# The late half of the diagonal: scored first and added on GpSimd instead of multiplied on its own

## The reference, cut to what matters

```
q, k = x @ Wq, latent_kv @ W_up_k ; v = latent_kv @ W_up_v      # B = 2, S = 1024, D = 128
scores = einsum('bhqd,bhkd->bhqk', qh, kh) * scale
scores = scores * exp(-0.0001 * |q_pos - k_pos|)                # decay by distance
out    = einsum('bhqk,bhkd->bhqd', softmax(scores), vh)
```

## Time and profile before

| what | value |
|---|---|
| median of 3 runs | 1040.08 us |
| the runs | 1040.08, 1025.58, 1045.73 us |
| the profiled execution | 1036.77 us, its span 1035.1 us |
| mean granted TensorE clock | 0.858 of full speed |
| busy in the span | PE 803.2, PEld 471.5, DVE 646.0, ACT 452.2, POOL 206.9 us |
| layer 0's attention groups | about 99 to 515 us of the span |

### The profile page before, as it was taken

How to read it: one execution, slowest core, us unless ns; L and a number is a source line. 1 busy time by engine, 2 the same in 40 slices (tenths; PEclk the granted TensorE clock), 3 DMA queues, 4 the chain that set the end, 5 groups by cost and what they waited for, 6 DMA issues and landing times. The chain is left out here.

```text
span 1035.1 us, 22868 instructions
## 1 busy us (share of the span) xinstructions
PE 803.2 (78%) x9457; PEld 471.5 (46%) x9457; DVE 646.0 (62%) x1922; ACT 452.2 (44%) x646; POOL 206.9 (20%) x218
## 2 busy tenths in 40 slices
PE   6374998999989999999754765999997793137960
PEld 3001554455545555554443653666664362025750
DVE  3784787689877989891053144667676545742427
ACT  5510576477757677778731232334332312001210
POOL 3980121111212121122204420000000000025330
PEclk9555799699989999999975887999999896558985
DMA  6535105031423231000084113700000001001014
GB/s 187 144 136 136 52 8 90 2 68 32 63 35 55 44 60 40 4 3 4 3 261 120 33 60 119 240 2 1 1 1 0 3 1 41 0 19 39 21 31 116
DMA packets 46217, 58.76 MB, mean 57 GB/s; under 512 B 7540, under 2 KB 24893, under 8 KB 46112
## 3 DMA queue, kind: packets, MB, share of 16 engines
q1 hardware_dynamic: 42992, 51.47, 19.2%
q0 software_dynamic: 2304, 4.59, 1.6%
q10 hardware_dynamic: 816, 1.23, 0.4%
HBM read 42.07 MB, written 14.94 MB: 55 GB/s over the span
## 5 line engine op out<-in xcount | busy, mean ns | idle before, releaser
L821 DVE CUSTOM_DVE_ANT_0 junk<-row,rest 128x512 bf16<-128x512 f32 x448 | 295.4, 691 | 62.8 <-PE row L421 61.8
L641 ACT ACTIVATE prob<-score 128x1024 f32<-128x1024 f32 x256 | 253.2, 1026 | 107.1 <-PE score L421 106.9
L421 PE MATMUL row<-stack 72*32 72x512 bf16 x1792 | 183.2, 399 | 5.1 <-issue 3.0
L421 PE MATMUL score<-stack 75*32 75x512 bf16 (+3 forms) x2816 | 163.2, 332 | 18.7 <-DMA stack<-neg_rows 9.8
L509 PE MATMUL out_ps<-prob,v_aug 128*32 128x256 f32 x2048 | 157.7, 392 | 0.0
L421 PEld LDWEIGHTS score<-stack 75*32 75x32 bf16 x2816 | 69.2, 98 | 86.9 <-issue 19.7
L722 POOL TENSOR_SCALAR_AFFINE_SELECT prob<-prob 128x512 f32<-128x512 f32 x64 | 40.7, 636 | 303.4 <-ACT prob L641 303.4
L421 PEld LDWEIGHTS row<-stack 72*32 72x32 bf16 x1792 | 48.7, 97 | 67.5 <-DVE top L821 44.0
L509 PEld LDWEIGHTS out_ps<-prob,v_aug 128*32 128x32 f32 x2048 | 62.7, 114 | 34.0 <-issue 4.9
L1393 PE MATMUL up_ps<-rows_t,up_w 128*128 128x320 f32 (+1 forms) x192 | 64.4, 465 | 14.0 <-issue 7.0
L1845 PE MATMUL outs<-vm_w,mixed 128*128 128x256 f32 x256 | 62.4, 387 | 1.8 <-issue 1.7
(11 more groups left out here) (298 smaller groups left out, 1132.1 us busy)
## 6 DMA issues: line engine op xcount, KB each, us to landing
stack<-parts_dram SPq DMA_DIRECT2D x288, 64.0 KB
parts_dram<-prob SPq DMA_DIRECT2D x12, 256.0 KB, 2.2
parts_dram<-stack SPq DMA_DIRECT2D x12, 256.0 KB, 3.5
results<-empty SPq DMA_DIRECT2D x12, 256.0 KB, 3.4
up_w<-in_L_ffn_w_dram SPq DMA_DIRECT2D x1, 2048.0 KB, 11.1
rows<-x_tok SPq DMA_DIRECT2D x8, 256.0 KB, 3.3
rows_in<-results SPq DMA_DIRECT2D x8, 256.0 KB, 4.2
up_w<-in_L_ffn_wg_dram SPq DMA_DIRECT2D x1, 2048.0 KB, 12.1
```

Source lines behind the costliest of these rows:

```text
L421: last = pe.matmul(out[c:c + 32, :], keys[:, c:c + 32], queries, start=True, stop=True)
L641: act.activation(prob[tile % 2][:, h, :], score[n % 2][:, :], ACT.Exp).then_inc(exped, 1)
L821: dve.tensor_tensor_reduce(junk[:, n % 2, :], row[:, n % 2, :], rest[:, at:at + HALF], 1.0, LOWEST, ALU.mult, ALU.max, top[:, 0, h, tile, ...
```

## The change

The late unit of a pair is put ahead of the pair's eight tile units. Its masked blocks are no longer multiplied by the values on PE. POOL masks a tile's diagonal blocks as before and then adds the pair's masked late blocks into them (fp32, 128 x 512 a tile, into `prob`), and signals `joined`. The tile's last weighing turn waits for `joined` in place of `masked`; ACT's next write to the late buffer waits for `joined` in place of the late product. `weigh_late` and its schedule entries go, so the schedule has 69 steps and NW is 8.

```diff
         for pair in range(SB // 2):
+            units += [("late", pair, 0)]
             units += [("tile", 2 * pair + k, h) for k in range(2) for h in range(GH)]
-            units += [("late", pair, 0)]
...
-            if kind == "tile" and tile > 1 and tile % 2 and h == 0:
-                schedule.append(("late", tile // 2 - 1, 0))
-        tail = [("weigh", SB - 1, turn) for turn in range(4)] + [("late", SB // 2 - 1, 0)]
+        tail = [("weigh", SB - 1, turn) for turn in range(4)]
...
-        NW = len(product_order)
+        NW = SB
...
-        def used_late(g, pair):
+        def joined_late(g, pair):
             if pair >= 2:
-                return g.n * NW + product_order.index(("late", pair - 2)) + 1
-            return (g.n - 1) * NW + product_order.index(("late", SB // 2 - 2 + pair)) + 1
+                return g.n * SB + 2 * (pair - 2) + 2
+            return (g.n - 1) * SB + 2 * (SB // 2 - 2 + pair) + 2
...
                     if turn == 3:
-                        pe.wait_ge(masked, g.n * SB + tile + 1)
+                        pe.wait_ge(joined, g.n * SB + tile + 1)
...
-                def weigh_late(g, pair):
-                    pe.wait_ge(mask_late, g.n * (SB // 2) + pair + 1)
-                    for k in range(2):
-                        tile = 2 * pair + k
-                        for h in range(GH):
-                            last = pe.matmul(out_ps[32 * h:32 * h + 32, tile * P:(tile + 1) * P],
-                                             v_aug[g.third][:, tile, h, :], prob_late[pair % 2][:, k, h, :],
-                                             start=False, stop=(pair == SB // 2 - 1), skip_group_check=True)
-                    last.then_inc(weighted, 1)
...
                             if not (first(g) and tile < 2):
-                                act.wait_ge(weighted, used_late(g, tile))
+                                act.wait_ge(joined, joined_late(g, tile))
...
+                        elif h == GH - 1:
+
+                            block = prob[tile % 2][:, :, tile * P:(tile + 1) * P]
+                            pool.wait_ge(exped, g.n * NU + n + 1)
+                            pool.affine_select(out=block, in_=block, compare_op=ALU.is_ge, fill=0.0, base=0,
+                                               pattern=[[0, GH], [1, P]], channel_multiplier=-1).then_inc(masked, 1)
+                            pool.wait_ge(mask_late, g.n * (SB // 2) + tile // 2 + 1)
+                            pool.wait_ge(masked, g.n * SB + tile + 1)
+                            pool.tensor_tensor(block, block, prob_late[tile // 2 % 2][:, tile % 2, :, :], ALU.add).then_inc(joined, 1)
```

More of the change, by code:

```diff
@@ L215, in attention @@
         neg_in = [sem(f"neg_in{i}") for i in range(3)]
-        scored, exped, masked, mask_late = sem("scored"), sem("exped"), sem("masked"), sem("mask_late")
+        scored, exped, masked, mask_late, joined = sem("scored"), sem("exped"), sem("masked"), sem("mask_late"), sem("joined")
         weighted, o_copied, o_turned, o_inv, o_done = sem("weighted"), sem("o_copied"), sem("o_turned"), sem("o_inv"), sem("o_done")
@@ L277, in attention @@
                      for key, order in orders.items()}
-        product_order = [(kind, tile) for kind, tile, turn in schedule + tail if kind == "late" or (kind == "weigh" and turn == 3)]
-        product_order = [("tile" if kind == "weigh" else kind, tile) for kind, tile in product_order]
-        NW = len(product_order)
+        NW = SB
         def used_tile(g, tile):
             if tile >= 2:
-                return g.n * NW + product_order.index(("tile", tile - 2)) + 1
-            return (g.n - 1) * NW + product_order.index(("tile", SB - 2 + tile)) + 1
-        def used_late(g, pair):
+                return g.n * NW + tile - 1
+            return (g.n - 1) * NW + SB - 1 + tile
+        def joined_late(g, pair):
             if pair >= 2:
-                return g.n * NW + product_order.index(("late", pair - 2)) + 1
-            return (g.n - 1) * NW + product_order.index(("late", SB // 2 - 2 + pair)) + 1
+                return g.n * SB + 2 * (pair - 2) + 2
+            return (g.n - 1) * SB + 2 * (SB // 2 - 2 + pair) + 2
         def judged_first(eng):
@@ L510, in weigh @@
                                          v_aug[g.third][:, tile, h, :], prob[tile % 2][:, h, at:at + S // 4],
-                                         start=(tile == 0 and turn < 2), stop=False, skip_group_check=True)
+                                         start=(tile == 0 and turn < 2), stop=(tile == SB - 1 and turn >= 2), skip_group_check=True)
                     if turn == 3:
                         last.then_inc(weighted, 1)
-                def weigh_late(g, pair):
-                    pe.wait_ge(mask_late, g.n * (SB // 2) + pair + 1)
-                    for k in range(2):
-                        tile = 2 * pair + k
-                        for h in range(GH):
-                            last = pe.matmul(out_ps[32 * h:32 * h + 32, tile * P:(tile + 1) * P],
-                                             v_aug[g.third][:, tile, h, :], prob_late[pair % 2][:, k, h, :],
-                                             start=False, stop=(pair == SB // 2 - 1), skip_group_check=True)
-                    last.then_inc(weighted, 1)
                 def turn_out(g):
@@ L552, in body @@
                                 turn_neg(nxt)
-                        elif kind == "weigh":
+                        else:
                             weigh(g, tile, h)
-                        else:
-                            weigh_late(g, tile)
                 run_groups(pe, body)
@@ L623, in finish @@
                 def finish(g):
-                    act.wait_ge(weighted, (g.n + 1) * (SB + SB // 2))
+                    act.wait_ge(weighted, (g.n + 1) * NW)
                     if not first(g):
@@ L717, in body @@
                     for n, (kind, tile, h) in enumerate(units):
[L718 to L724, removed]
                         if kind == "late":
```

## The result

| | median of 20 runs | lowest to highest |
|---|---|---|
| before | 1032.72 us | 1020.92 to 1047.85 |
| changed | 1036.74 us | 1026.93 to 1045.12 |

A forecast was written before the change was run, and what follows sets the result against it. PE was taken as the bound at full clock, with DVE only 6% behind. The terms -6.3 + 2.1 + 0.7 + 0.9 + 1.4 gave -1.2 us, 1035.6 on the profiled run, forecast at 1037; 8-in-10 range 1020 to 1051.

The forecast's parts named there:

- My own sign of being wrong: At a group's end, output copy beginning later than T + 8.5 us, T being the last row unit on PE.
- the groups of 58 rows: Four groups with 58 row units, each forecast 1.1 us shorter (4.4 in all) as late products leave PE.
- DVE's two-input instructions: POOL's add slows two subtractions in DVE's negated-maxima chain: +0.2 us a group, 7 times, +1.4; row maximum priced 0.
- The end of a group: From the last row unit to the output copy, the cover hiding the late mask is used up: +0.1 us, 7 groups, +0.7.
- Late products leave PE: 32 late products of 0.44 us leave PE, 14.1 at most; DVE's row pacing leaves -6.3 us together.
- The late unit at the start: Pair 0's late unit is new at a group's start, where exponentials outlast PE's step: 0.3 x 7 = +2.1 us.
- The last group: ACT ends it; after the last exponential, mask, add, waits and product take 2.8 us against 1.86 before: +0.9.
- POOL's add: 1.27 us each, 64 times, 81 us on POOL, 10 a group: hidden, with 30 us to spare.
- rival 3: The add also holds DVE's row maximum (line 821): about +70 us, 1106; chance 0.04.
- Rival 1: Full gain: doubled row units fill holes in DVE, nearly all 14.1 us come off, 1023 to 1027; chance 0.16.
- Rival 4: The extra late unit's wait and the joins eat all gain and more: +1 us a group, 1045; chance 0.05.
- Rival 2: PE's unexplained stalls, guessed as instructions running dry behind stack loads, move: 1019 without both, 1053 with two more; chance 0.15.

The follow-up runs named there:

- e1: The changed kernel with POOL's add for tile 6 held until DVE has finished the negated maxima; ratio to the kernel before 1.0022 (0.9978 to 1.0065).
- e8: The changed kernel with tile 6's add replaced by a one-input POOL mask of about the same length; no total time or ratio given.
- e11: The kernel before with a one-input POOL copy of 896 columns added across DVE's negated-maxima steps in each group but the last; ratio 1.0001 (0.9953 to 1.0049).
- e3: The changed kernel without POOL's add, the masked late blocks left out of the result; ratio 0.9981 (0.9949 to 1.0013).
- e2: The kernel before with the late unit at the start of its pair, late products still on PE, no add; ratio 1.0005 (0.9961 to 1.0050).
- e12: The kernel before without the stack loads of groups 3 to 7; ratio 0.9913 (0.9873 to 0.9952).
- e5: The kernel of e1 with tile 7's late blocks multiplied on PE instead of added by POOL; ratio 0.9996 (0.9964 to 1.0028).
- e4: The changed kernel with RESERVE 11 in place of 13, row units spread over 58 of 69 steps; ratio 1.0060 (1.0019 to 1.0100).
- e6: The kernel of e5 with RESERVE 12, the last row unit one step later; ratio 1.0107 (1.0051 to 1.0163).
- e10: The kernel before, unchanged, run again for a second trace; against itself in that comparison 0.9953 (0.9917 to 0.9988).

## Why the prediction was wrong

Forecast: -1.2 us on the profiled execution. Undisturbed groups say about +0.15 in kind A (-0.2 against the second trace of the kernel before, 52.57), +0.4 in B and +0.85 in C, twice each, +0.55 for the last, and in the first group's end +1.4 (copy at T + 8.73 in place of T + 7.35), which its stretch before T may partly give back (its length hangs on how long the clock stayed low at the start, and differed by 11 us between traces): 2.7 to 4.8 us. The medians differ by 4.0. The timed intervals are +4.1 to +10.5 us and -0.8 to +7.5; if the first is taken at its middle, 2 to 5 us of it are not explained by the groups. My own sign of being wrong, a copy later than T + 8.5, came true (8.95); the groups of 58 rows, which I had about 1 us shorter, are 0.4 to 0.85 longer. Step by step:

- *DVE's two-input instructions: the step that failed in its mechanism.* I priced +0.2 a group, through two subtractions, and said that the transpose had 0.3 of room. The instruction held was the cast between them, with one input in SBUF (the subtraction behind it kept its 0.19), and the transpose came 0.57 late, all of it paid by the group: 4 us in place of 1.4 (e1, e8, e11). I had taken from the row-maximum rows that one SBUF input is safe. Those rows show that for an instruction that reads PSUM and SBUF, and nothing for casts and tensor_scalars within SBUF. The Trainium skill's page "SBUF — State Buffer", section "Who interferes with whom", has this case: an instruction with one SBUF input keeps clear of GpSimd only outside the 2-port modes; copy, cast and tensor_scalar can run in such a mode, and then whichever of VectorE and GpSimd issues first blocks the other fully until it ends. The traces agree: the casts and the tensor_scalar that started behind POOL lasted until POOL's end (1.14, 0.95 and 1.12 us in place of 0.18). In which mode they ran no run shows.
- *The end of a group: mis-sized.* I compared with T + 8.04, which is kind A's. The ends before were 8.04, 8.43 and 7.75, and 7.35 in the first group. Without the cast's part (e1) they are 8.38, 8.38 and 8.15, and 8.15: +0.34, -0.05, +0.4, +0.8, together 2.2 us in place of 0.7. In e1 the last exponential ended at T + 5.5, where I had 5.3, and the copy came 2.9 behind it, where I had 2.6.
- *Late products leave PE: right in kind, too large.* In seven groups 3 to 3.6 us came off (e3 against e2), where my figures give 5.0 for the same seven and 6.3 for all with the stretches at half clock. That DVE's row pacing holds the rest fits: in kind B up to T, PE's row loads waited 6.7 us for DVE in e3, 5.1 in e2. The miss is in kinds B and C, where the part from the copy to T shrank by 0.62 us and I had 1.1; in kind A it shrank by 0.7 in one group and 0.1 in the other, and I had 0.3.
- *The late unit at the start:* +0.47 before T in each group where I had 0.3, but most of it came back at the end (e2), +0.1 to +0.2 a group in all.
- *The last group:* +0.55 in place of +0.9.
- *POOL's add:* 1.28 us, hidden, the row maximum untouched: right, and rival 3 is out. (Its sum had an error: 81 us less 448 times 0.04 is +63, not +70.) Rival 1 is out too: without any add e3 was at best 5 us below the kernel before by its timed interval. Rival 4, which I gave 0.05, is the one that came, smaller than its +1 a group. Rival 2: the stalls are real, move from run to run, and are what I took them for (e12). In the four traces of the two kernels they do not account for the difference; in the timed runs this was not measured.

Of PE's busy time I said 1.7 us a group less. It fell by 0.8 to 0.9 in undisturbed groups; I read this as overlap, since products that overlap leave less busy time than their starts suggest.

## What to carry to other kernels

Before moving work to GpSimd, list what VectorE runs at that moment in SBUF alone: casts, copies and scalar steps of 0.2 us wait out a GpSimd instruction of 1.3 us, and a short chain on the critical path is where that hurts, however idle GpSimd looks. Count such a chain's room in each kind of loop body, not in one. And where two engines are within 6% of each other, taking work from one gains what the other leaves: here 3 to 3.6 of 12.3 us, less than the 4 that one new wait at each group's end took back.

## What the runs showed of the hardware

- A GpSimd instruction that reads and writes SBUF held DVE's cast (fp32 to bf16) and tensor_scalar, both of 128x32 and within SBUF, until it ended: 0.79 to 1.15 us in place of 0.18. An add with two inputs, a mask with one and a copy with one all did so. A tensor_scalar that had started 0.02 us before the add kept its 0.18. The 128x512 maximum with one input from PSUM was not held (690 ns).
- PE's waits within a group for nothing that the profile shows, 1 to 3.6 us, came behind late packets of the queue of kind "instruction": 10 to 15 us apart in place of about 7, while the stack loads ran. PE went on 2.6 to 3.3 us after the late packet's start, in all 16 cases. Without those loads neither the gaps nor the waits were there (e12). Such a gap did not always make PE wait (e3, e5: gaps of 11 to 14 us, no wait of 1 us).
- The granted clock fell to 0.5 (1.2 GHz) behind some of PE's waits and not behind others: for 17 us from the last microsecond of the 3.26 us wait of the kernel before, for 17 us behind one of 0.67 us in e4, for 10 to 24 us behind those of 0.94 to 1.40 us in e6, and not at all behind the 0.67 us in e5 or the 1.75 us in the changed kernel.
- It also fell to 0.5 in the last group of three traces (the changed kernel, e1, e10), 5 to 6 us behind its start, and cost 1.6 us. In the changed kernel PE had stood 0.16 to 0.35 us for ACT before each of four units just ahead of it. In other traces of the same kernels it did not fall.
